# Audio tower, attention over channels: the third chunk of weights is turned with the first two, the fourth with the queries and keys

## The reference

```python
weight = einsum('bct,bcs->bts', q * scale, k * scale)      # 512 x 512 per sequence
weight = softmax(weight, axis=-1)
h = einsum('bts,bcs->bct', weight, v)                      # 125 x 512
h = h + attn(layernorm(h))       # 8 heads, 2 key/value heads, rotary, tanh cap of 50
h = h + ffn(layernorm(h))        # shared SwiGLU + top 2 of 8 experts
```

## Time and profile before

| | us |
|---|---|
| median of 3 runs | 5851.24 (5850.75 to 5853.52) |
| the profiled execution | 5854.09 |
| its span, first to last instruction | 5852.4 |
| TensorE matmul busy in it | 5718.3 |
| VectorE, ScalarE, GpSimd busy | 4162.2, 3386.4, 2073.7 |
| mean granted TensorE clock | 0.991 |

### The profile page before, as it was taken

One profiled execution on the slowest core, in us unless ns is written; L12 is line 12 of the kernel. 1 busy time (PEld: TensorE's weight loads), 2 busy tenths in 40 slices (PEclk: granted clock), 3 DMA queues, 4 the chain that ended last, 5 costly groups with the idle time before them and its releaser, 6 DMA issues. The chain is left out here.

```text
span 5852.4 us, 109659 instructions
## 1 busy us (share of the span) xinstructions
PE 5718.3 (98%) x32259; PEld 5031.6 (86%) x32259; DVE 4162.2 (71%) x9591; ACT 3386.4 (58%) x6260; POOL 2073.7 (35%) x1711
## 2 busy tenths in 40 slices
PE   5999999999999999999999996999999999999999
PEld 4888888888888888888888885999999999999998
DVE  3777777777777777777777775666666766676765
ACT  4666666666666666666666663555555555555554
POOL 1333333333333333333333332334344433444343
PEclk8999999999999999999999998999999999999999
DMA  2111111111111111111111111677777777777762
GB/s 74 45 50 47 44 50 46 44 51 46 45 51 45 45 50 45 46 51 44 46 50 44 46 50 60 180 187 186 187 187 185 185 186 184 184 186 184 188 163 79
DMA packets 363663, 565.45 MB, mean 97 GB/s; under 512 B 92898, under 2 KB 187106, under 8 KB 363492
## 3 DMA queue, kind: packets, MB, share of 16 engines
q1 hardware_dynamic: 294276, 433.22, 24.7%
q0 software_dynamic: 69344, 131.70, 11.3%
HBM read 438.14 MB, written 138.42 MB: 99 GB/s over the span
## 5 line engine op out<-in xcount | busy, mean ns | idle before, releaser
L1429 POOL DMA_INDIRECT out_dram<-res,goal x273 | 553.0, 2026 | 1068.8 <-DMA entries<-routed_entries 481.5
L945 POOL TENSOR_TENSOR vT_low<-vT_full,vT_high 128x500 fp32r<-128x500 f32 x128 | 163.1, 1274 | 1576.5 <-ACT vT_high L691 1576.5
L624 ACT ACTIVATE e<-ps,negmax 128x512 f32<-128x512 f32 x512 | 350.9, 687 | 426.9 <-PE ps L437 415.5
L1179 PE MATMUL ps<-rT_hi,up_hi 128*128 128x384 f32 x2548 | 552.2, 338 | 1.6 <-DVE rT_lo L1339 1.6
L1179 PE MATMUL ps<-rT_lo,up_hi 128*128 128x384 f32 x2548 | 552.4, 338 | 0.0
L1179 PE MATMUL ps<-rT_hi,up_lo 128*128 128x384 f32 x2548 | 551.7, 338 | 0.0
L1269 ACT ACTIVATE uT_hi<-egb 128x384 fp32r<-128x384 f32 x364 | 191.4, 526 | 572.1 <-DVE egb L1358 561.5
L966 POOL DMA_INDIRECT routed_entries<-entry,slot x256 | 320.4, 1252 | 467.8 <-DVE slot L906 425.4
L1179 PEld LDWEIGHTS ps<-rT_hi,up_hi 128*128 128x128 f32 x2548 | 457.7, 188 | 9.9 <-issue 2.0
L1179 PEld LDWEIGHTS ps<-rT_lo,up_hi 128*128 128x128 f32 x2548 | 456.4, 188 | 0.0
L1179 PEld LDWEIGHTS ps<-rT_hi,up_lo 128*128 128x128 f32 x2548 | 456.1, 188 | 0.0
(11 more groups left out here) (220 smaller groups left out, 15034.2 us busy)
## 6 DMA issues: line engine op xcount, KB each, us to landing
raw<-in_L_ffn_w SPq DMA_DIRECT2D x182, 768.0 KB, 5.0
X<-in_x SPq DMA_DIRECT2D x128, 750.0 KB
raw<-in_L_ffn_w SPq DMA_DIRECT2D x91, 896.0 KB
raw<-in_L_ffn_w SPq DMA_DIRECT2D x273, 128.0 KB, 5.0
normed_rows<-y SPq DMA_DIRECT2D x128, 250.0 KB
out_dram<-h SPq DMA_DIRECT2D x128, 250.0 KB
rows<-normed_rows,entries POOLq DMA_INDIRECT x273
out_dram<-res,goal POOLq DMA_INDIRECT x273
```

What stands on the lines that cost most here:

```text
L624: nc.scalar.activation(e[:, i, :], ps[:, (i + 1) % 2, :], ACT.Exp, bias=negmax[:, i:i + 1], accum_out=total[:, i:i + 1]).then_inc(e_sb.sem, 1)
L1179: ins = nc.tensor.matmul(ps[:, bank, 0:GROUP], w[a][:, k, col:col + P], rT[b][:, k, :], start=(k == 0 and i == 0), stop=(k == KC - 1 and i ...
L1429: nc.gpsimd.indirect_dma_start(out, bass.IndirectOffsetOnAxis(ap=goal[group[1] % 2][:, i:i + 1], axis=0), res[i][:], None, bounds_check=la ...
```

## The change

`turn_weights(2)` moves up, directly behind chunks 0 and 1, and `turn_weights(3)` down, behind the down product and the counting matmuls, directly ahead of the turns of `rc`. A table gives the banks: chunk 2 goes to bank 6, chunk 3 to bank 1. With the banks go the waits. Chunk 2 waits until both halves of the small attention have been read (`attn_sb`). The down product, which writes into bank 6, waits for three splittings (`e_lo.at(t, 3)`) in the place of `attn_sb`. The blend into bank 0 waits for one splitting instead of three. On ScalarE and VectorE rounding and splitting of chunk 2 move up to those of 0 and 1.

```diff
--- before.py
+++ after.py
@@ -367,6 +367,7 @@
         RANKS = D - 2 * E
         CAPF = 50.0
         TANH = 1.0 / (16.0 * CAPF)
+        E_BANK = (0, 1, 6, 1)
 
         with nc.Block() as block:
             @block.sync
@@ -442,10 +443,12 @@
 
                         if j == 0:
                             pe.wait_ge(e_norm.sem, e_norm.at(t))
-                        elif j >= 2:
-                            pe.wait_ge(e_lo.sem, e_lo.at(t, j - 1))
+                        elif j == 2:
+                            pe.wait_ge(attn_sb.sem, attn_sb.at(f))
+                        elif j == 3:
+                            pe.wait_ge(e_lo.sem, e_lo.at(t, 2))
                         for i in range(KC):
-                            last = nc.tensor.transpose(ps[:, j % 2, i * P:(i + 1) * P], e[:, i, j * P:(j + 1) * P],
+                            last = nc.tensor.transpose(ps[:, E_BANK[j], i * P:(i + 1) * P], e[:, i, j * P:(j + 1) * P],
                                                        ident[:])
                         last.then_inc(eT_ps.sem, 1)
 
@@ -515,6 +518,7 @@
                     if has(0):
                         turn_weights(0)
                         turn_weights(1)
+                        turn_weights(2)
                     if has(1):
 
                         pe.wait_ge(tanh_sb.sem, tanh_sb.at(f))
@@ -523,12 +527,9 @@
 
                         pe.wait_ge(aT_hi.sem, aT_hi.at(f))
                         product(pe, ps[0:C, 7, :], aT, woT, P, 0, D, aT_lo.sem, aT_lo.at(f)).then_inc(wo_ps.sem, 1)
-                    if has(0):
-                        turn_weights(2)
-                        turn_weights(3)
                     if has(3):
 
-                        pe.wait_ge(attn_sb.sem, attn_sb.at(f))
+                        pe.wait_ge(e_lo.sem, e_lo.at(t, 3))
                         pe.wait_ge(hT_hi.sem, hT_hi.at(g))
                         for part in range(2):
                             for k in range(3):
@@ -546,6 +547,8 @@
                                          start=True, stop=True)
                         nc.tensor.matmul(ps[:, 3, RANKS + E:RANKS + 2 * E], ones16[0:C, :], m16[0:C, :],
                                          start=True, stop=True).then_inc(rank_ps.sem, 1)
+                    if has(0):
+                        turn_weights(3)
                     if has(1):
 
                         pe.wait_ge(rope_add.sem, rope_add.at(a))
@@ -560,7 +563,7 @@
                     if has(0):
 
                         pe.wait_ge(vT_lo.sem, vT_lo.at(t))
-                        pe.wait_ge(e_lo.sem, e_lo.at(t, 3))
+                        pe.wait_ge(e_lo.sem, e_lo.at(t, 1))
                         for j in range(KC):
                             pe.wait_ge(e_hi.sem, e_hi.at(t, j + 1))
                             for b in range(2):
@@ -628,7 +631,7 @@
                     def weights_hi(j):
                         act.wait_ge(eT_ps.sem, eT_ps.at(t, j + 1))
                         act.wait_ge(o_ps.sem, o_ps.at(a))
-                        nc.scalar.activation(e_cut[0][:, j, :], ps[:, j % 2, :], ACT.Copy).then_inc(e_hi.sem, 1)
+                        nc.scalar.activation(e_cut[0][:, j, :], ps[:, E_BANK[j], :], ACT.Copy).then_inc(e_hi.sem, 1)
 
                     def soften(kv):
 
@@ -686,13 +689,13 @@
                     if has(0):
                         weights_hi(0)
                         weights_hi(1)
+                        weights_hi(2)
                         act.wait_ge(vT_sb.sem, vT_sb.at(t))
                         act.wait_ge(o_ps.sem, o_ps.at(a))
                         nc.scalar.activation(vT[0][:, :, :], vT_full[:, :, :], ACT.Copy).then_inc(vT_hi.sem, 1)
                     if has(-1):
                         round_scores(back(t, -1))
                     if has(0):
-                        weights_hi(2)
                         weights_hi(3)
                     if has(1):
                         act.wait_ge(rT_ps.sem, rT_ps.at(a))
@@ -734,7 +737,7 @@
                     def weights_lo(j):
                         dve.wait_ge(e_hi.sem, e_hi.at(t, j + 1))
                         dve.wait_ge(o_ps.sem, o_ps.at(a))
-                        nc.vector.tensor_tensor(e_cut[1][:, j, :], ps[:, j % 2, :], e_cut[0][:, j, :].bitcast(F32),
+                        nc.vector.tensor_tensor(e_cut[1][:, j, :], ps[:, E_BANK[j], :], e_cut[0][:, j, :].bitcast(F32),
                                                 ALU.subtract).then_inc(e_lo.sem, 1)
 
                     def normalise(kv):
@@ -833,6 +836,7 @@
                     if has(0):
                         weights_lo(0)
                         weights_lo(1)
+                        weights_lo(2)
                     if has(1):
 
                         dve.wait_ge(rT_ps.sem, rT_ps.at(f))
@@ -862,7 +866,6 @@
                         alone(dve)
                         nc.vector.bn_aggr(ag2[0:C, :], st2[0:C, :]).then_inc(ag2_sb.sem, 1)
                     if has(0):
-                        weights_lo(2)
                         weights_lo(3)
                     if has(2):
```

## The result

| | before | after |
|---|---|---|
| median of 4 runs each, us | 5852.38 | 5993.18 |
| ratio, 95% interval | | 1.0238 (1.0225 to 1.025) |
| profiled execution, us | 5854.09 | 5996.45 |
| its span, us | 5852.4 | 5994.7 |

The change costs 141 us. The forecast was +70 us and 5921 us with a range from 5886 to 5939: the direction was right, the size half of what came, and the measured time lies 54 us above the range. The granted clock, 0.991, is that of before.

A forecast was written before the change was run, and what follows sets the result against it. TensorE, gapless in a steady step, was taken as the bound. Two waits, the second absorbing the first, cost 0.54 us a step: 125 x 0.54 = 67.5, plus 2.5 for filling, +70, 5921 us; range 5886 to 5939.

The forecast's parts named there:

- What bounds the kernel: Steady step: TensorE has 27.38 us of matmul in 27.38 us, no gap, so any wait is paid in full.
- The run that goes away: TensorE's turns: two runs a step instead of three, the fourth chunk joining the query and key turns; -0.07 us a step.
- The wait at down: TensorE's down product waits for VectorE's third splitting, starting at 2040.94 instead of 2040.71; with 0.11 restart loss, late by 0.34 us.
- The wait for POOL's addition: TensorE's turns of rotated queries and keys wait for POOL, starting 0.43 us later; with 0.11 more behind it, 0.54 a step.
- the loss of the five turns behind this wait: Five turns of queries and keys on TensorE take 0.60 us after a wait against 0.49: 0.11 more, other bound 0.
- Behind that nothing more is late: Rest of the step: fourth rounding, fourth splitting, y and qkT_lo arrive in time, 0.4 us of slack at queries and keys.
- only the wait for the bank: Rival: POOL's addition is in time, leaving only down's wait; 0.27 us a step, +36, 5887 us; chance 0.12.
- no wait, one run saved: Rival: third splitting done when down wants its weights, TensorE gapless; -0.07 a step, -6, 5845 us; chance 0.05.
- Another deadline breaks: Rival: y or fourth splitting half a microsecond later uses up slack at queries and keys; 0.2 gives 5946 us; chance 0.05.
- The clock did not fall: Rival on TensorE's clock: waits drop it to 0.68 for 9 us each step, losing 2.9 us, 6281 us; chance 0.03.
- VectorE's added splitting: Ahead of VectorE's rotation: holds it back 0.60 us by the trace; 0.69 by the cited rule, which would give 5932 us.
- if a third place waits: Sign in the changed profile that the forecast is wrong: TensorE waits somewhere besides down and the query and key turns.

## Why the prediction was wrong, point by point

- **What bounds the kernel:** right. TensorE had no gap, and every wait went into the time.
- **The run that goes away, -0.07 a step:** wrong, it is 0 (1.0, 0.9991 to 1.0009, with one run more). I took the product's late second start for a cost of the run and did not look at the distance from the last turn to the first product. In the sum the term hardly counted, since the second wait swallows it.
- **The wait at down:** right in place and cause. Down started 0.15 to 0.23 late (1.08 and 1.16 less the 0.93 of four products), for 0.23 forecast. The loss behind its start is the 0.11 of the forecast: 0.81 for the first three products (2033.33 to 2034.14), 0.70 where nothing waits.
- **The wait for POOL's addition:** right, and it absorbs the first (5909.9 with the first wait, 5910.4 without it). The two together measure 56 us; the forecast had 70. The term that was too large is the loss of the five turns behind this wait: 0.51 us (2036.63 to 2037.14), so 0.02 over the 0.49 and not 0.11. The turns of rc came 0.40 to 0.48 later against the turns of attn, for 0.43.
- **"Behind that nothing more is late":** this is the step that failed, and in it the sentence that POOL's scatters "were not waited for". y was worked out as one microsecond late, which came out nearly right (1.2), and I followed it to its turns and to qkT_lo, not to POOL's split and what stands behind that in POOL's order: the scatters, the root, xn and gb, for which the attention product of the next step waits. It is worth 83 of the 141 us. The rows for it were at hand: an entry row of 1.12 us for 8 columns, ending with POOL's split, and xn waiting for a root that is issued behind two scatters.
- **The rivals:** both first waits are there, so neither "only the wait for the bank" nor "no wait, one run saved" came. "Another deadline breaks" had the right form at the wrong deadlines, at 0.05 and with a price of 25 us. The clock did not fall: 1.00 in the steps with three waits. VectorE's added splitting took 0.60, the time between starts, and not 0.69: three in a row take 1.80 to the next instruction (2031.39 to 2033.19), two took 1.21. The section that the prediction cites against this, The DRAIN you can't avoid on the page VectorE: DVE Perf Modes of the Trainium skill, goes on that a next operation which is not held starts earlier, so the prediction was wrong to call the trace a disagreement with it.
- **The signs:** of those that were to show the forecast wrong, "if a third place waits" is the one that came.

## What to carry to other kernels

When an instruction is made late, follow it on every queue it enters, past its reader: what stands behind the reader in that engine's order is late too, up to the next step, where the loop closes. Read spare time from the end of the producer to the earliest start that was ever seen behind it, not to the start in a run that did not wait. And before counting the end of a run of short matmuls as a cost, add up the whole stretch in a kernel that has one run more.

## What the hardware showed that I had not expected

- POOL's elementwise work on SBUF stops some of VectorE's instructions until it is over, and the time appears as duration of the VectorE row, not as idle time: 0.34, 1.12, 1.52 us for the same 8 columns, which take 0.15 with no such work beside them, and 2.41 for y instead of 0.54. Instructions that take one operand from PSUM ran beside it at their normal 0.68. The Trainium skill, page SBUF — State Buffer, section Who interferes with whom, says that a VectorE instruction with two SBUF inputs contends with a GpSimd instruction that reads SBUF, and that with VectorE in a two-port mode the one that issues first holds the shared ports for its whole instruction. The traces agree for the entry row, which has two SBUF inputs. For y, which has one SBUF tensor and two columns of scalars, they show the hold, but not in which mode it ran.
- From the slots' end to the start of the first scatter it is 0.97 us (2043.58 to 2044.55), and the two scatters take 1.30 and 1.21 on POOL with 0.30 between them. A root that needs 1.0 us stands behind 2.8 us of them.
- Fp32 turns of 128 columns are 0.108 us apart at the 2.4 GHz level (0.76 for seven distances).
